# A mixture in two parts, a reordered start, and gathers placed between writes in a fused conv and expert kernel

## The reference

```
cond0: h = gelu(gelu(cond @ W0 + b0) @ W1 + b1); att = softmax(h @ W2 + b2)        # 128 x 8
       agg_w[b] = sum_k att[b, k] * weight[k]       # a 32 x 32 matrix for each batch row
       y = agg_w[b] @ x[b] + (att @ bias_k)[b]
ffn0:  gates = softmax of the top 2 of 4 of y @ Wr.T
       x1 = x + 4 * sum_e gates_e * (y @ A_e.T) @ B_e.T                             # 4 experts, rank 16
cond1: o = conv1d(x1, 9 taps, 4 groups of channels) + ctx[b, c] + side[c]
ffn1:  hidden = relu(layernorm(o @ gw1.T + gb1) * gamma + beta); gates = hidden @ gw2.T + gb2
       top 2 of 8, softmax, an expert over its capacity is switched off
       x2 = x1 + o @ weight.T + (1/16) * sum_e w_e * (o @ lora_A_e) @ lora_B_e
```

## Time and profile before

| | us |
|---|---|
| median of 3 runs (316.31 to 319.11) | 316.49 |
| the profiled execution's time | 317.21 |
| its span | 315.4 |
| TensorE busy | 294.3 (93%) |
| VectorE busy | 198.1 (63%) |
| ScalarE busy | 124.7 (40%) |
| GpSimd busy | 97.5 (31%) |

### The profile page before, as it was taken

The page is one execution under the profiler, slowest core; times in us unless marked ns, Lnnn a source line. Parts: engine busy times, 40 slices in busy tenths (PEclk is TensorE's granted clock), DMA queues, the critical chain, the costliest instruction groups (busy, mean ns, idle before and its releaser), DMA issues.

```text
span 315.4 us, 6197 instructions
## 1 busy us (share of the span) xinstructions
PE 294.3 (93%) x2015; PEld 242.6 (77%) x2015; DVE 198.1 (63%) x503; ACT 124.7 (40%) x261; POOL 97.5 (31%) x127
## 2 busy tenths in 40 slices
PE   7999989989998999999989999999999899898994
PEld 6999867658886888778867887788777777686882
DVE  1369764633749464946493749474958455878785
ACT  4424535423822382238223822382227326112330
POOL 5345215114211421142114121412112226216660
PEclk9999999999999999999999999999999999999999
DMA  5968399694299439943984299429644980004887
GB/s 133 282 100 270 120 243 220 184 203 100 108 281 177 104 120 267 181 100 121 277 166 103 84 289 190 99 94 241 129 101 153 222 158 0 0 2 150 326 326 268
DMA packets 74024, 52.76 MB, mean 167 GB/s; under 512 B 44156, under 2 KB 61004, under 8 KB 74000
## 3 DMA queue, kind: packets, MB, share of 16 engines
q1 hardware_dynamic: 72752, 51.75, 64.9%
q10 hardware_dynamic: 848, 0.55, 0.7%
q0 software_dynamic: 400, 0.16, 0.3%
HBM read 35.67 MB, written 16.78 MB: 166 GB/s over the span
## 4 chain that ended last, share of the span: by engine, by line
PE 62%; DMA 14%; DVE 10%; ACT 5%; issue 4%; SPq 2%; POOL 0%; DVEq 0%; ACTq 0%; POOLq 0%
DMA xg<-x1d 12%; PE ps_g L1093 10%; PE ps_d L1093 9%; PE ps_a L1054 8%; PE ps_c L1228 7%; PE ps_a L1043 4%; PE ps_t L1244 3%; DMA x1d<-xq 2%; PE ps_d L1269 2%; ACT xq L602 2%; ACT xT L553 2%; PE ps_d L1114 2%; PE ps_d L1270 2%; PE ps_v L1066 1%; PE ps_d L1436 1%
## 5 line engine op out<-in xcount | busy, mean ns | idle before, releaser
L489 POOL TENSOR_TENSOR o1l<-o,o1h 128x512 fp32r<-128x512 f32 x30 | 39.3, 1311 | 156.8 <-ACT o L614 156.8
L1093 PE MATMUL ps_d<-wt_hi,o1h 128*128 128x336 f32 (+1 forms) x120 | 41.1, 342 | 0.3 <-DVE y_all L929 0.3
L1228 PE MATMUL ps_c<-xg,cw 96*32 96x512 f32 x256 | 34.1, 605 | 5.4 <-DMA xg<-x1d 5.4
L1093 PE MATMUL ps_d<-wt_hi,o1l 128*128 128x336 f32 (+1 forms) x120 | 38.7, 323 | 0.0
L1093 PE MATMUL ps_d<-wt_lo,o1h 128*128 128x336 f32 (+1 forms) x120 | 38.6, 322 | 0.0
L923 DVE TENSOR_TENSOR oT<-ps_c,biasT 128x512 f32<-128x512 f32 x32 | 21.9, 685 | 24.3 <-PE ps_c L1228 24.3
L602 ACT ACTIVATE xq<-y_all 128x512 f32 (+1 forms) x29 | 32.2, 1138 | 11.5 <-DVE y_all L929 7.9
L1093 PE MATMUL ps_g<-wt_hi,o1h 128*128 128x336 f32 x112 | 35.6, 318 | 0.5 <-ACT tmp_all L629 0.4
L1093 PE MATMUL ps_g<-wt_hi,o1l 128*128 128x336 f32 x112 | 35.5, 317 | 0.0
L1093 PE MATMUL ps_g<-wt_lo,o1h 128*128 128x336 f32 x112 | 35.3, 315 | 0.0
L1054 PEld LDWEIGHTS ps_a<-pm,xT 128*128 128x128 f32 x256 | 29.7, 192 | 0.6 <-ACT xT L553 0.5
(11 more groups left out here) (244 smaller groups left out, 591.8 us busy)
## 6 DMA issues: line engine op xcount, KB each, us to landing
xg<-x1d SPq DMA_DIRECT2D x64, 254.0 KB, 4.6
xg<-x1d SPq DMA_DIRECT2D x32, 256.0 KB, 3.4
x1d<-xq SPq DMA_DIRECT2D x30, 256.0 KB, 2.1
xs<-in_x_dram SPq DMA_DIRECT2D x6, 1024.0 KB, 8.3
out_dram<-xT SPq DMA_DIRECT2D x16, 256.0 KB, 2.1
out_dram<-xg SPq DMA_DIRECT2D x16, 256.0 KB, 2.5
y_all<-in_x_dram SPq DMA_DIRECT2D x1, 1024.0 KB, 7.7
y_all<-in_L_ffn_weight_dram SPq DMA_DIRECT2D x1, 1024.0 KB, 6.9
```

Of the source, the lines that this page charges most:

```text
L489: pool.tensor_tensor(lo, o1[t % 2][:, :, :], hi.bitcast(fp32), ALU.subtract).then_inc(s_o1l, 1)
L1093: last = T.matmul(bank[:, 0:columns], a[:, Q - 1 - q, :], w[:, q, first:first + columns], start=(q == 0 and n == 0), stop=(q == Q - 1 and ...
L1228: last = T.matmul(ps_c[C * g:C * g + C, :], cw[0:KC, g, :, :].rearrange("p q o -> p (q o)"), xg[0:KC, t % 2, :, g, :], start=True, stop=True)
```

## The change

- **SyncE, steps 1 to 7:** the gather of tile 0 goes between writes 1 and 2, after a wait for write 0's landing. Before, it stood behind all four writes (in step 0 it was between them already).
- **The mixture in two parts:** step 0's 16 batch rows are made first, by 8 products over all 128 rows of the array with the attention spread in strips (`attD`); VectorE makes `mixbd` of step 0 from PSUM. The other 112 rows come in `mixture(1)` and `mixture(2)`, 16 products each, the first among step 1's transposes, the second after x1 of step 0. `mix_all` gets only rows 16 to 127. The weight load `wk` is interleaved in o (strips o = 4*o' + j).
- **TensorE's start:** 18 `keep_busy` less (one before the attention product, three before the mixture, 8 and 3 around gm_transposed(0), 4 before u_products(2), against one put in before mix(0); one of two moves behind two transposes). b's transposes go between u products; the gate weights' transposes go to ps_v behind step 1's; w_transposed(0) and (1) go behind delta(0,3) and among step 2's transposes; u_products(2) goes behind conv(0,0).
- **ScalarE:** u_out(0) first, then the bias, gate0_exp(0) before x_transposed(1), copies of the mixture between; w_hi(0) and (1) go behind x1_reorder(0, 2), w_hi(2) and (3) behind x_transposed(2).
- **VectorE:** b's split before `mixbd`, `gw1` after x1 of step 0, all four w_lo in a row before gates0(1).
- **GpSimd:** only bias_mixed(0) in the start, the eight small norm loads behind it; mixing(1) behind the two x1 copies of step 0.
- **Loads:** A and Wr of ffn0 (`aw`) go from GpSimd's queue to SyncE's, the second half of x step 0 from SyncE's to ScalarE's, x step 1 behind b on SyncE's; b's rows are read as (p c).

```diff
 SyncE
             for j in range(4):
                 sp.dma_start(wk[C * j:C * j + K0],
-                             mixw[:, MO * j:MO * (j + 1)].rearrange("k o i a -> k o (i a)"))
+                             mixw.rearrange("k (o j) i a -> j k o (i a)", j=4)[j])
-            sp.dma_start(xs_early[0][:, NT // 2:NT, :], ...)
+            sp.dma_start(aw[0:ER0], ...); sp.dma_start(aw[ER0:UC], ffr)
             sp.dma_start(mbn, row(mixb, 1, BT))
-            sp.dma_start(xs_early[1], x_v[1]).then_inc(s_x1st, 16)
             for e in range(E0):
-                ... ffb[e].rearrange("(c p) r -> p c r", p=P)
+                ... ffb[e].rearrange("(p c) r -> p c r", c=HC)
+            sp.dma_start(xs_early[1], x_v[1]).then_inc(s_x1st, 16)
 ...
-                    for t in range(NT):
-                        write(s, t)
+                    write(s, 0)
+                    write(s, 1)
                     if at_step(s, 1):
                         sp.wait_ge(s_cp, 3)
+                    wait(sp, s_x1w[0], (s + 1) * 16)
                     gather(s, 0)
+                    write(s, 2)
+                    write(s, 3)
                     wait(sp, s_x1w[2], (s + 1) * 32)
 GpSimd
             pool.wait_ge(s_const, 4)
-            pool.wait_ge(s_msa, MG // 2)
-            pool.wait_ge(s_msd, MG // 2)
             pool.wait_ge(s_mbsb, 1)
-            mixing(0)
+            pool.wait_ge(s_ss["rs"], 1)
+            bias_mixed(0)
             ... norm loads
-            mixing(1)
 ...
                         (x1 copies of tiles 1 and 3)
+                    mixing(1)          # its product waits for s_msa 6 and s_msd 2
                     pool.wait_ge(s_gah, 1)
 ScalarE
             x_transposed(0)
+            u_out(0)
             act.wait_ge(s_sp["bias"], 1)
             ... biasT
-            (four copies of the mixture)
-            u_out(0)
+            gate0_exp(0)
             x_transposed(1, (0, 1))
-            gate0_exp(0)
+            mix_copied(1, 2)
+            mix_copied(1, 3)
             x_transposed(1, (2, 3))
+            mix_copied(1, 0)
+            mix_copied(1, 1)
 ... step -1
-                    w_hi(0)
-                    w_hi(1)
                     gm_out(0)
                     x1_reorder(0, 0)
                     u_out(1)
+                    mix_copied(2, 0)
+                    mix_copied(2, 2)
+                    x_transposed(2, (0, 1))
+                    x1_reorder(0, 2)
+                    w_hi(0)
+                    w_hi(1)
+                    x_transposed(2, (2, 3))
                     w_hi(2)
                     w_hi(3)
-                    x_transposed(2, (0, 1))
-                    x1_reorder(0, 2)
                     gate0_exp(1)
-                    x_transposed(2, (2, 3))
 VectorE
+            V.tensor_tensor(attD, row(ps_v[:, 0:N0], 1, 4), row(repmask[:, :], 2, N0), ALU.mult)
             (attT, pm)
-            (four copies of the mixture)
+            b_hi, b_lo from ps_t
+            dve.wait_ge(s_mp0, 1)
+            V.tensor_tensor(mixbd, ps_c..., repmask..., ALU.mult).then_inc(s_bd, 1)
             (mixbias, rs)
-            b_hi, b_lo; gw2bd, ga
             gates0(0)
 ... step -1
-                    w_lo(0)
-                    w_lo(1)
                     for t in range(NT):
                         x1_out(0, t, xs_early[0])
+                    gw2bd, ga
+                    for j in (1, 3):
+                        dve.wait_ge(s_mps, 2)
+                        V.tensor_copy(mix_home(2, j), mix_part(j)).then_inc(s_msd, 1)
                     (three copies to cw)
-                    w_lo(2)
-                    w_lo(3)
+                    for q in range(Q):
+                        w_lo(q)
                     gates0(1)
 TensorE
+            u_products(0, (0,))
             (b's transposes)
-            u_products(0)
+            u_products(0, (1,))
+            pe.wait_ge(s_attD, 1)
+            for o in range(MO):
+                last = T.matmul(ps_c[:, o * 4 * N0:(o + 1) * 4 * N0],
+                                wkr[:, o, :, :].rearrange("k r i -> k (r i)"),
+                                attD.rearrange("p j n -> p (j n)"), start=True, stop=True)
+            last.then_inc(s_mp0, 1)
             (mixbias, rs)
+            u_products(0, (2, 3))
+            pe.wait_ge(s_bd, 1)
+            keep_busy(1)
             mix(0)
+            (bias)
+            def mixture(part): 16 products, moving attT[C * j:C * (j + 1), N0:NB] into ps_m[j]
+            t1(1, ..., 0); t1(1, ..., 1); mixture(1); t1(1, ..., 2); t1(1, ..., 3)
+            (gw1, gw2 into ps_v); u_products(1, (0,))
 ... step -1
-                    keep_busy(8, ps_v)
                     gm_transposed(0)
-                    u_products(1, (2,))
-                    keep_busy(3, ps_v)
+                    u_products(1, (1,))
                     delta(0, 0)
                     delta(0, 1)
-                    u_products(1, (3,))
+                    u_products(1, (2,))
                     delta(0, 2)
                     delta(0, 3)
-                    w_transposed(2)
-                    w_transposed(3)
-                    mix(1)
-                    (step 2's transposes)
-                    keep_busy(4)
-                    u_products(2)
+                    u_products(1, (3,))
+                    pe.wait_ge(s_x1, NT)
+                    mixture(2)
+                    x_third(0); x_third(1)
+                    w_transposed(0)
+                    w_transposed(1)
+                    x_third(2); x_third(3)
+                    mix(1)
+                    w_transposed(2)
+                    w_transposed(3)
                     pe.wait_ge(s_wlo, Q)
                     conv(0, 0)
+                    u_products(2)
                     gm_transposed(1)
```

More of the change, by code:

```diff
@@ L174, in adaln_ffn_kernel @@
         attT = early(P, [P])
+        attD = early(P, [4, NT * BT])
         sm = early(P, [4])
@@ L1185, in _ @@
             last.then_inc(s_sp["b"], 1)
[L1186 to L1193 removed]
+            u_products(0, (1,))
+            pe.wait_ge(s_attD, 1)
+            pe.wait_ge(s_ss["wkr"], 1)
+            for o in range(MO):
[3 more added lines that the diff above has]
+            last.then_inc(s_mp0, 1)
+            pe.wait_ge(s_ld["mixb"], 16)
+            pe.wait_ge(s_ss["attT"], 1)
+            T.matmul(ps_v[:, P:P + NB], mbn.rearrange("k r o -> k (r o)"), attT[0:K0], start=True, stop=True)
+            for c in range(HC):
+                last = T.matmul(ps_v[:, RS0:RS0 + UC], ones[:, :], pm[:, c, :],
+                                start=(c == 0), stop=(c == HC - 1))
+            last.then_inc(s_mbps, 1)
+            u_products(0, (2, 3))
+            pe.wait_ge(s_bd, 1)
+            keep_busy(1)
             pe.wait_ge(s_mbsb, 1)
@@ L1196, in _, with mixture @@
             mix(0)
-            pe.wait_ge(s_x1st, 16)
-            for t in range(NT):
-                if t == 0:
-                    pe.wait_ge(s_u, 1)
-                pe.wait_ge(s_xt, NT + max(t - 1, 0))
-                t1(1, xs_early[1], t)
+            pe.wait_ge(s_ss["b"], 1)
+            T.transpose(ps_t[:, 0:NB], bex, idp).then_inc(s_sp["bias"], 1)
+            def mixture(part):
+                for o in range(4):
+                    for j in range(4):
+                        last = T.matmul(ps_m[j][:, o * (NB - N0):(o + 1) * (NB - N0)],
+                                        wkr[C * j:C * (j + 1), 4 * part - 4 + o, :, :].rearrange("k r i -> k (r i)"),
+                                        attT[C * j:C * (j + 1), N0:NB], start=True, stop=True)
+                last.then_inc(s_mps, 1)
+            pe.wait_ge(s_x1st, 16)
+            pe.wait_ge(s_xt, NT)
+            t1(1, xs_early[1], 0)
+            t1(1, xs_early[1], 1)
+            pe.wait_ge(s_ss["ctx"], 1)
+            mixture(1)
+            for t in (2, 3):
+                pe.wait_ge(s_xt, NT + t - 1)
+                t1(1, xs_early[1], t)
+            pe.wait_ge(s_ld["gate"], 32)
+            pe.wait_ge(s_v, 1)
+            for q in range(Q):
+                last = T.transpose(ps_v[:, q * G1:(q + 1) * G1],
+                                   gw1n.rearrange("p (m q) -> p q m", q=Q)[:, q, :], ident[0:G1, 0:G1])
+            T.transpose(ps_v[:, Q * G1:Q * G1 + E1], gw2n.rearrange("e t c -> e (t c)"),
+                        ident[0:E1, 0:E1]).then_inc(s_sp["gw1"], 1)
             def w_transposed(q):
```

147 lines of the change are left out of this document (66 added, 81 removed).

## The result

The changed kernel takes 321.37 us, median of 9 runs (318.84 to 323.17); the kernel before, run beside it, 317.51 (316.31 to 319.11, 9 runs). The ratio is 1.0115, 95% interval 1.0071 to 1.0159: slower by about 1.2%, outside my range (309.5 to 317.0) and on the side to which I had given 0.08. (In all that follows medians are over every run, while ratios leave out runs that stand over 1.5% above their kernel's fastest, which takes five of e6's ten runs out of its ratio, three each of e2's and e5's, and two of e9's. Each batch has its own runs of the kernel before, with medians of 317.5 to 318.8 us, so kernels of different batches are compared by their ratios.)

A forecast was written before the change was run, and what follows sets the result against it. TensorE, busy 93% of the span, was taken as the bound. -4.7 (gathers) and +0.4 (start) gave -4.3 on the profiled 317.21 us: 312.9, or 312.2 as median; range 309.5 to 317.0.

The forecast's parts named there:

- Part 3: From x1(0,3) through gates0(1) to main(0,0): the start's gain is lost again, main(0,0) at 51.6 against 51.16, +0.4 us.
- Part 1: SyncE, steps 1 to 7: gathers between the writes cut TensorE's waits for `xg`, -4.7 us, between 0 and -5.0.
- The terms for conv(2,1), (4,1) and (7,0): Steps 2, 4 and 7: earlier gathers cut the waits of these convolutions by 0.8, 1.3 and 0.8 us.
- the give-back: Rival: writes 2 and 3 queue behind the gather, conv(s,1) waits instead of conv(s,0); time 316.2, chance 0.24.
- Part 2: The start up to gates0(0): v at 21.5, gates0(0) ending at 27.1, x1(0,3) ready at 32.1.
- the stretch of 1.4: In gates0(0): VectorE operations beside GpSimd's norm DMA issues take 1.4 us longer, ending at 27.1.
- The rule that I had set against the row: In gates0(0): by the skill page no stretch, end at 25.7; the forecast went by the row, 27.1.
- conv(0,0) waits for w_lo(3): Before conv(0,0): the convolution starts once VectorE's w_lo(3) is done, at 40.4.
- it has 1 us of cover left: u_products(2), moved behind conv(0,0), runs 41.5 to 45.0, done before gm_T(1) with 1 us to spare.
- The clock rival: Start, from 38: TensorE's granted clock falls to 1.2 GHz for ten microseconds, +7.7 us, time 319.9; chance 0.10.
- the sign to look for: u_products(2) taking over 4 us would show that the clock had fallen in the start.

The follow-up runs named there:

- e6: Kernel before without its keep_busy(8), keep_busy(3) and keep_busy(4) in step -1; 320.67 us, ratio 1.0008.
- e2: Changed kernel with u_products(2) back in front of conv(0,0); 316.83 us, ratio 0.9940.
- e5: Changed kernel with the two x loads (steps 2 and 3) issued ahead of the lora_A loads on SyncE; 319.33 us, ratio 1.0021.
- e9: Changed kernel with the x load of step 3 moved from ahead of write(0,0) to behind gather(0,1); 317.83 us, ratio 0.9998.
- e12: Changed kernel with x of step 3 behind gather(0,1), gather(s,1) waiting for write 1 alone, and keep_busy(6) before conv(0,0); 312.10 us, ratio 0.9834.
- e3: Kernel before with only the gather of tile 0 put between writes 1 and 2 in steps 1 to 7; 314.98 us, ratio 0.9875.
- e7: Kernel before with the gathers between the writes and gather(s,1) waiting for write 1 alone, ahead of the x load; 311.88 us, ratio 0.9817.
- e1: Changed kernel with keep_busy(14) in the idle between w_transposed(3) and conv(0,0); 314.60 us, ratio 0.9884.
- e8: Changed kernel with x ahead of lora_A, gather(s,1) after write 1 alone, filler around conv(0,0) and u_products(2) and before the hidden transpose; 312.52 us, ratio 0.9818.
- e10: Changed kernel with x of step 3 behind gather(0,1) and gather(s,1) waiting for write 1 alone, no filler; 317.41 us, ratio 0.9986.
- e4: Changed kernel with the gather of tile 0 behind all four writes again; 324.73 us.
- e11: Kernel before with gathers between the writes, gather(s,1) waiting for write 1 alone, and keep_busy(8) before the last hidden transpose; 312.12 us, ratio 0.9823.

## Why the prediction was wrong, step by step

**The steps that failed.** The first is in Part 3: TensorE's products between w_transposed(3) and main(0,0) were counted at full clock, with u_products(2) done before gates0(1), and the fall of the clock was left to a rival with a chance of 0.10. The clock stood at 0.50 there and main(0,0) came 5.80 us later than in e12. The second is in Part 1: that writes 2 and 3 land later was put at nothing. conv(1,0) and conv(1,1) waited 3.12 us.

**Part 1, forecast -4.7.** The terms for conv(2,1), (4,1) and (7,0) held, 3.04 us of waits gone. The step that failed is "writes 2 and 3 go out up to 0.5 us later and their packets stand behind the gather's", costed at nothing: gather(1,1) waits for them, and conv(1,1) waited 2.69 (1.25 in e3). Besides, write(1,0) was taken to land in 4.87 us as before, and took 6.33. The changed kernel gained 1.48 behind main(0,0) where -4.7 was forecast, e3 3.35. e7, where gather(s,1) no longer waits for writes 2 and 3, gained 4.66. My argument against the give-back, that gather(s,1) hangs on a convolution, did not hold for step 1, and for later steps only in some runs: none of them waits in the changed kernel's, but conv(4,1) still waits 0.95 in e2's, and conv(7,1), which did not wait before, 0.99 in e9's.

**Part 2, right up to x1, and sooner.** v(0) came at 21.17 (forecast 21.5), gates0(0) ended at 25.49 (27.1), x1(0,3) at 30.91 (32.1). The miss of 1.6 is the stretch of 1.4 that I took from a row, and v(0) 0.3 sooner; gates0(0) took 4.32, the 4.3 of the forecast without stretch. (The forecast's 27.1 and 25.7 are each 0.1 short of their own terms, 21.5, 4.3 and 1.4.) In the changed kernel the same operations run beside the same issues and are not stretched:

```profile
21.43 1.96 POOL L493 DMA_DIRECT2D betaT<-in_L_ffn_ln_beta_dram  x4
```

```profile
21.85 0.17 DVE L784 TENSOR_TENSOR sc<-v,small 128x16 f32<-128x16 f32 x1
21.94 0.22 DVE L786 TENSOR_TENSOR pair<-v 128x64 f32<-128x64 f32 x1
22.19 0.23 DVE L787 TENSOR_TENSOR pair<-pair,upper 128x64 f32<-128x64 f32 x1
```

The rule that I had set against the row, the Trainium skill, page SBUF — State Buffer, section Who interferes with whom (two SBUF inputs contend with a GpSimd instruction that reads SBUF, not with one that only writes), gave 25.7, and the trace has 25.49. In gates0(1) the rule's other half is seen: a product with two SBUF inputs took 1.55 us at 40.89, beside GpSimd's split of 1.54 at 40.87, where it takes 0.18 otherwise. What stretched the operation at 24.22 in the earlier trace rows stays open.

**Part 3, the copies right, the cover wrong.** w_hi(3) ended at 38.43 (39.7), w_lo(3) at 39.15 (40.4), gates0(1) at 44.73 (46.0): each 1.2 to 1.3 early, as x1 was. With the clock held, main(0,0) starts at 51.00 to 51.07 in e1, e8 and e12, -0.1 to -0.2 where I had +0.4. Two sentences failed. "conv(0,0) waits for w_lo(3)": in the changed kernel it waited for gather(0,0), 1.6 us longer. I had moved x1(0,0), and with it write(0,0), ahead by 4 us and never asked what stood in front of it on SyncE's queue; the issues of the x loads and their 2 MB were in the trace of before, where the write came late enough to miss them. And, of u_products(2), "it has 1 us of cover left": at half clock it takes 3.3 us more, and even at full clock, in e1, the late gather moved its end to 45.80, 1.1 us behind the end of gates0(1) at 44.72.

**The clock rival, right in mechanism, wrong in chance and in its terms.** It had the place (37 to 40.4, only w_transposed(2) and (3)), the point from which it decides (u_products(2) ending after 46; it ended at 49.8), and the sign to look for (over 4 us; it took 7.10). It priced the work ahead of main(0,0) at 4 us and main(0,0) itself at 3.7. The first measured 5.80 (against e12), the second nothing, since the clock was back at 54.5, ahead of 56.80. Its total, 319.9 against 321.37 measured, came near by luck, because the 3.12 us of conv(1,0) and (1,1) took the place of the 3.7. I gave it 0.10 since the longest idle at full clock in the earlier trace rows was 2.02 and here there would be 1.0 and 1.4. That comparison failed: the 2.02 lies in the steady part, between long products, these idles among transposes and small products, without the filler. In e9 the clock fell there behind an idle of 1.61.

The Trainium skill, page TensorE: Matmul & The Clock Gate, section What's actually happening, says that the throttled level is the default and that activity releases it. These runs agree in kind: the thin stretches of the changed kernel and of e9 are followed by 0.50, the filled one of e12 is not. I had the sentence in hand and used it for a tenth.

## What to carry over

When a step is moved sooner, look at what stands ahead of it on its DMA queue at the new moment, and at who waits for the landing; a write or gather that was late enough to find the queue empty may now stand behind megabytes. When work is taken from TensorE ahead of a chain of products, look at how thin the work gets over the stretch and not only at its longest idle; where it is thin, a few products that nobody reads are worth trying first, since here 1.5 us of them bought 3.7 us at main(0,0). And a wait should name the transfer that it needs: gather(s,1) needs write 1, and waiting for writes 2 and 3 gave back 1.3 of the 4.7 us that the new order brings (3.35 in e3 against 4.66 in e7).

## What the runs showed of the hardware that I had not expected

**The length of an idle does not say whether the clock falls.** 1.61 us before conv(0,0) was followed by a fall in e9 and e10; in the same place of the last step, 1.56 us before the hidden transpose was followed by one in e10 (274.6 to 278.0) and by none in e12.

**Low stretches differ in length.** Behind a single idle in the dense part the clock came back soon (70.2 to 73.6 in e1, 279.8 to 283.2 in the changed kernel), and so it did at two places of the start (46.6 to 50.0 in e2, 31.1 to 34.5 in e6). In the start with u_products(2) behind conv(0,0) it stayed low for 10.2 us (e10), 13.7 (changed kernel, e9) and 20.5 (e4), though TensorE shows as busy 12.22 of 13 us. All the long ones have u_products(2), with its 68-column products, in them; whether that is the reason was not tested.

**The scatter of runs goes in part with the clock.** The kernel before ran from 315 to 322 us in 61 ordinary runs of the experiments' batches, with mean clocks from 1.000 to 0.979, the four quickest at 0.998 to 1.000 and the six slowest at 0.979 to 0.988. But eleven runs with the same mean of 0.995 still lie between 316.5 and 319.1 us, so something else scatters too. e7, e8, e11 and e12, which are at 0.996 or more in all but one run, stay within some 1.4 us but for that run (314.44 at 0.989) and one far outlier, 1595.11 us at a recorded clock of 1.000, whose cause is not known.
